# A two-layer graph network on one core: three more tiles of the last block columns kept in SBUF during the first sweep

## The chip, the cores and the metric

The kernel runs on one core of a Trainium2 chip. The metric is device time in microseconds of one execution, as the median of several runs. TensorE (PE) multiplies, VectorE (DVE) and ScalarE (ACT) work on SBUF and PSUM, the queues of SyncE (SP) and GpSimd (POOL) issue the DMA transfers.

## What is computed

```python
x = layernorm(x + layer0(x)); x = layernorm(x + layer1(x))          # x is 8192 x 128
# layer0: d = adj.sum(1); s = 1/(sqrt(d)+1e-8); (adj * s[:,None] * s[None,:]) @ (x@W0 + b0)
# layer1: a = adj + eye;  s = 1/sqrt(a.sum(1)); relu((a * s[:,None] * s[None,:]) @ (x@W1) + b1)
```

`adj` is 8192 x 8192 in float32 (268 MB). Both layers scale it by the degrees of its rows and columns, so a product with column j of the matrix needs the degree of row j first, and layer 1 needs the normalised rows that layer 0 makes.

## The kernel before

**Tiles.** The matrix is cut into 16 x 16 tiles of 512 x 512 (1 MB each), called (i, j). Row i is read in order of i in sweep 1. All tiles of the upper triangle are read again in sweep 2 and all others in sweep 3: 256 + 120 + 136 loads, whatever the constants are.

**Sweep 1** sums the rows for the degrees and multiplies for layer 0 what it can, in f32 (L659). A left tile (j < i) finds its features ready. A tile at or right of the diagonal has to wait until the degree of row j is known. Some are held for that: `held(j)` is min(j, NEAR[j]), so with NEAR = 3 the diagonal tile of column j and the three above it stay in SBUF and are multiplied, by `scaled_takes(j)`, after row j is complete and two tiles of row j + 1 are done. `early(i, j)` says whether a tile is a left tile or a held one. The tiles further right are *far*: ACT only adds them up (L711), from the layout `adj_far`, and their slot is free again. DVE sums all others (L817), folds the row (L824, L827), TensorE turns the sums (L595), and DVE and ACT make the scale and then the features of the row (L835 to L856).

**Sweep 2** goes over the rows from 14 down to 0, each from the last column to the one right of the diagonal. A take of layer 1 (`right1`) needs x1 of row j, the output of layer 0; a far tile is multiplied for layer 0 too (`late0`), in the same take. ACT casts each half of a tile to a high float32r part (L702), DVE makes the low part (L806), and TensorE multiplies three times for each quarter (L683, L684, L685): 12 matmuls for one layer, 24 for both. **Sweep 3** does the left and diagonal tiles for layer 1, and writes the output. I call the takes of sweep 2 t0, t1 and so on: t0 is (14, 15), t1 and t2 are (13, 15) and (13, 14), t6 is (11, 15), t10 and t11 are (10, 15) and (10, 14), t15 is (9, 15).

**From layer 0 to layer 1.** For each row from 15 down: its sums come to SBUF, by ACT's copy out of the bank (L739) if no far tile is outstanding, else the part of sweep 1 was stored in DRAM by L534, is loaded again (L549), and the rest is added by DVE (L872). Rows with a far tile are `late_rows`, here 11 to 0. TensorE turns the sums (`turn0`, L607), DVE makes h and its moments (L884 to L786), ACT the root (L744), DVE x1 (`make_x1`, L774 to L795), TensorE turns x1 (`turn1`, L618), ACT copies it (L747), TensorE multiplies by the weights (`features1`, L626), ACT makes the high part of the features (L751) and DVE the low part (L900). `split_high` and `split_low` (L718, L864) split the f32 features of layer 0, column by column, before the first far tile of that column comes.

**Order.** The class `Plan` writes out the order of each engine's work before the kernel is built: every operation has a key, in units of loads, and each engine runs its list sorted by key; all engines are in-order. `pe_before[u]` is what TensorE does ahead of take u. `turn0[i]` stands 2 takes behind the last product of the row's sums and at least 2 behind the turn before it, `turn1[i]` 3 takes behind `turn0[i]`, the features one further, none later than its first use. PSUM has 6 banks for sums; a group of sums holds its bank from its first take until it is copied out, and `held_before` says which load was in a slot before. Sweep 1 has 19 slots for tiles, 3 of its own (`own`) and 16 that lie where features and rings of later sweeps come (`lent`); sweep 2 only has the 3, and the casts have a ring of 4 halves, so the cast of a take waits until the take two before it is multiplied.

Of the kernel before, what the change touches and what calls it, by code (L numbers as in the profile page):

```python
# [9 lines left out]
NB = N // T  # L10
TILE = Q * T
HALF = TILE // 2
HQ = Q // 2
NEAR = [3] * NB
FAR_PARTS = 4
OWN_SLOTS = 3
LENT1_SLOTS = 16
# [17 lines left out]
def held(j):  # L35

    return min(j, NEAR[j])

# [940 lines left out]
```

How the kernel before makes its waits and increments, by code:

```python
        @block.sync  # L493
        def _(sp):
            sp.dma_start(w_sb[:, :], w0).then_inc(const_landed, 16)
            sp.dma_start(b_sb[:, :], b0.partition_broadcast(P)).then_inc(const_landed, 16)
            for n, (sweep, i, j) in enumerate(loads):
                if sweep < 2 and n % NB == 0:
                    if i >= 2:
                        sp.wait_ge(mixed0_done, i - 1)
                    sp.dma_start(x_t[:, i % 2, :], x_cols[:, i * T:(i + 1) * T]).then_inc(x_t_landed[i % 2], 16)
                m = plan.held_before[n]
                if m is not None:
                    if loads[m][0] == 0:
                        sp.wait_ge(far_summed, plan.far_summed[m])
                    elif loads[m][0] == 1:
                        sp.wait_ge(tile_summed, plan.summed[m])
                        sp.wait_ge(halves_used, 2 * plan.take_of[m] + 2)
                    else:
                        sp.wait_ge(low_ready, 2 * (plan.take_of[m] - plan.natives) + 2)
                elif plan.slot[n] >= OWN_SLOTS + LENT1_SLOTS:
                    sp.wait_ge(halves_used, 2 * plan.lent_again + 2)
                source = adj_far[plan.far_summed[n] - 1] if sweep == 0 else adj_tiles[i, j]
                sp.dma_start(raw(n), source).then_inc(tile_landed[plan.slot[n]], 16)
# [11 lines left out]
            def stored(layer, i):  # L526
                m = stage_at[("empty_right1" if layer else "empty_early0", i)]
                pool.wait_ge(sums_stored[m % 2], 16 * (m // 2 + 1))
```

## Time and profile before

| what | before |
|---|---|
| median of 3 runs | 1884.1 us (1882.98 to 1884.22) |
| the profiled execution | 1884.51 us, span 1882.3 us, mean clock 0.964 |
| TensorE busy | 1655.4 us (88%) |
| TensorE weight loads | 1117.6 us (59%) |
| DVE busy | 1264.2 us (67%) |
| ACT busy | 739.5 us (39%) |
| DMA | 573.38 MB, mean 305 GB/s |

A row of the chain or of the timeline gives the start, the duration and what ran, with how many instructions are merged; in brackets stands how long the engine had been idle and what ended it. PEclk is the granted TensorE clock as a share of full speed. Busy times of matmuls overlap, since they are pipelined.

### The profile page before, as it was taken

The numbers are of one execution on the slowest core, as the hardware profiler recorded it, in microseconds if no ns is written. First come the engines' busy times: TensorE is split into PE (matmuls) and PEld (weight loads), VectorE is DVE, ScalarE is ACT, GpSimd is POOL, SyncE is SP. The second block draws the span as 40 slices with busy tenths as digits, with TensorE's granted clock in tenths as the row PEclk, the third lists the DMA queues.
The fourth block names the chain that finished last, engine by engine and source line by source line (L and its number), as shares of the span: only waits on it lengthen the run. The fifth ranks groups of instructions, "written<-read, shape, count | busy, mean of one in ns | idle before, by whom it ended". The sixth has DMA issues, their size and how long they took to land.

```text
span 1882.3 us, 17109 instructions
## 1 busy us (share of the span) xinstructions
PE 1655.4 (88%) x6136; PEld 1117.6 (59%) x6136; DVE 1264.2 (67%) x1854; ACT 739.5 (39%) x889; POOL 66.2 (4%) x127
## 2 busy tenths in 40 slices
PE   0257889999999999968999999999999999999996
PEld 0123344444444444456777777787787787777775
DVE  1444556776876567277655656545547899999996
ACT  5553342111000000045444444444446666666663
POOL 0000000000000000000000000000000000000000
PEclk9778899999999999989999999999999999999998
DMA  9999999998877976155666665656567999999991
GB/s 387 421 421 421 421 422 393 416 404 343 366 312 290 367 298 232 28 213 212 250 232 227 229 227 209 213 219 228 196 216 313 421 397 363 353 356 361 362 367 78
DMA packets 85906, 573.38 MB, mean 305 GB/s; under 512 B 10400, under 2 KB 10656, under 8 KB 20288
## 3 DMA queue, kind: packets, MB, share of 16 engines
q1 hardware_dynamic: 76320, 541.23, 72.6%
q0 software_dynamic: 9504, 31.07, 4.7%
q8 instruction: 50, 0.82, 0.2%
q14 instruction: 32, 0.26, 0.0%
HBM read 556.79 MB, written 15.47 MB: 304 GB/s over the span
## 4 chain that ended last, share of the span: by engine, by line
PE 67%; DVE 18%; DMA 11%; issue 3%; ACT 1%; SPq 0%; DVEq 0%; POOL 0%; ACTq 0%
PE acc L659 28%; PE acc L683 12%; PE acc L685 12%; PE acc L684 12%; DVE low L806 7%; DMA lent<-adj_tiles 6%; DMA own<-adj_tiles 2%; DVE stats L781 1%; DMA own<-adj_far 1%; DMA lent<-adj_far 1%; DVE run L817 1%; DVE o L795 1%; PE turned L595 1%; DVE z L930 1%; DVE h L884 1%
## 5 line engine op out<-in xcount | busy, mean ns | idle before, releaser
L683 PE MATMUL acc<-high,feat_high 128*128 128x512 f32 x1336 | 536.1, 401 | 70.6 <-DVE low L806 59.5
L659 PE MATMUL acc<-lent,feat 128*128 128x512 f32 x1168 | 522.8, 607 | 20.9 <-DVE feat L856 13.5
L685 PE MATMUL acc<-high,feat_low 128*128 128x512 f32 x1336 | 526.7, 394 | 0.0
L684 PE MATMUL acc<-low,feat_high 128*128 128x512 f32 x1336 | 525.9, 394 | 0.0
L806 DVE TENSOR_TENSOR low<-own,high 128x1024 fp32r<-128x1024 f32 x330 | 390.5, 1220 | 177.7 <-ACT high L702 175.1
L702 ACT CAST high<-own 128x1024 fp32r<-128x1024 f32 x330 | 338.2, 1052 | 197.1 <-PE acc L685 190.4
L659 PEld LDWEIGHTS acc<-lent,feat 128*128 128x128 f32 x1168 | 226.2, 195 | 304.5 <-issue 288.6
L817 DVE TENSOR_TENSOR run<-run,lent 128x2048 f32<-128x2048 f32 x135 | 309.3, 2291 | 135.8 <-DMA lent<-adj_tiles 129.7
L683 PEld LDWEIGHTS acc<-high,feat_high 128*128 128x128 f32 x1336 | 254.1, 190 | 139.2 <-issue 81.5
L685 PEld LDWEIGHTS acc<-high,feat_low 128*128 128x128 f32 x1336 | 254.0, 190 | 55.2
L684 PEld LDWEIGHTS acc<-low,feat_high 128*128 128x128 f32 x1336 | 254.5, 191 | 50.1
L806 DVE TENSOR_TENSOR low<-lent,high 128x1024 fp32r<-128x1024 f32 x182 | 211.8, 1219 | 3.9 <-ACT high L702 2.0
L702 ACT CAST high<-lent 128x1024 fp32r<-128x1024 f32 x182 | 186.3, 1051 | 54.6 <-PE acc L685 52.9
L711 ACT ACTIVATE lent<-lent 128x2048 f32<-128x2048 f32 (+3 forms) x80 | 118.0, 1475 | 74.8 <-DMA lent<-adj_far 73.9
L722 ACT ACTIVATE root<-deg 128x8 f32<-128x8 f32 x16 | 3.3, 209 | 300.4 <-DVE deg L837 300.4
L731 ACT COPY stage<-acc 128x512 f32<-128x512 f32 x27 | 15.8, 586 | 260.7 <-PE acc L659 206.4
L595 PE MATMUL turned<-ones,rowsum 128*128 128x1 f32 x128 | 20.9, 284 | 108.1 <-DVE rowsum L827 108.1
L659 PE MATMUL acc<-own,feat 128*128 128x512 f32 x256 | 115.1, 600 | 0.0
L595 PEld LDWEIGHTS turned<-ones,rowsum 128*128 128x128 f32 x128 | 20.4, 243 | 109.7 <-DVE rowsum L827 67.4
L659 PEld LDWEIGHTS acc<-own,feat 128*128 128x128 f32 x256 | 48.9, 192 | 60.4 <-issue 60.4
L835 DVE TENSOR_REDUCE far<-far_parts 128x4 f32<-128x16 f32 x16 | 2.7, 169 | 108.7 <-PE turned L595 108.7
L817 DVE TENSOR_TENSOR run<-run,own 128x2048 f32<-128x2048 f32 x27 | 61.9, 2291 | 17.5 <-DMA own<-adj_tiles 15.8
(77 smaller groups left out, 649.3 us busy)
## 6 DMA issues: line engine op xcount, KB each, us to landing
lent<-adj_tiles SPq DMA_DIRECT2D x237, 1024.0 KB, 11.1
own<-adj_tiles SPq DMA_DIRECT2D x197, 1024.0 KB, 5.6
lent<-adj_far SPq DMA_DIRECT2D x60, 1024.0 KB, 23.0
own<-adj_far SPq DMA_DIRECT2D x18, 1024.0 KB, 23.0
x_in<-x_rows POOLq DMA_DIRECT2D x32, 256.0 KB, 4.4
sums_rows<-stage POOLq DMA_DIRECT2D x27, 256.0 KB, 6.4
sums_in<-sums_rows POOLq DMA_DIRECT2D x27, 256.0 KB, 6.3
x_t<-x_cols SPq DMA_DIRECT2D x16, 256.0 KB, 15.6
```

Of the source, the lines that this page charges most:

```text
L595: mm = nc.tensor.matmul(turned[:, q:q + 1], rowsum[:, q * P:(q + 1) * P], ones[:, :], start=True, stop=True)
L659: mm = nc.tensor.matmul(bank, feat0[:, j * Q + q, :], raw(n)[:, q * T:(q + 1) * T], start=(u == plan.first[g] and q == 0), stop=(u == plan ...
L683: nc.tensor.matmul(bank, f_high, a_high[:, chunk], start=(u == plan.first[g] and q == 0), stop=False)
L684: nc.tensor.matmul(bank, f_high, a_low[:, chunk], start=False, stop=False)
L685: mm = nc.tensor.matmul(bank, f_low, a_high[:, chunk], start=False, stop=(u == plan.last[g] and q == Q - 1))
L702: nc.scalar.copy(high(m), raw(n)[:, half * HALF:(half + 1) * HALF])\
L711: ins = nc.scalar.activation(piece, piece, ACT.Copy, accum_out=far_parts[:, r, q, k:k + 1])
L781: ins = nc.vector.bn_stats(stats[:, q, :], h[:, q, :])
L795: ins = nc.vector.tensor_scalar(dst[:, q, :], h[:, q, :], moments[:, q, 0:1], rstd[:, q:q + 1], ALU.subtract, ALU.mult)
L806: nc.vector.tensor_tensor(low(m), raw(n)[:, half * HALF:(half + 1) * HALF], high(m).bitcast(F32), ALU.subtract).then_inc(low_ready, 1)
L817: ins = nc.vector.tensor_tensor(run[:, :], run[:, :], raw(i), ALU.add)
L884: ins = nc.vector.scalar_tensor_tensor(out=h[:, q, :], in0=turned_q[:, q, :], scalar=scale[:, i, 0, q:q + 1], in1=x_in[:, r, q, :], op0=AL ...
```

## The change

One constant: the last two block columns hold four and five tiles above their diagonal.

```diff
-NEAR = [3] * NB
+NEAR = [3] * (NB - 2) + [4, 5]
```

So (10, 14), (10, 15) and (11, 15) are held and multiplied in sweep 1 by L659, summed by DVE and loaded in the layout of the other tiles, and in sweep 2 they are takes of layer 1 alone. Everything that `Plan` derives from `held`, `early` and `far_width` follows: rows 10 and 11 have no far tile and are no `late_rows`, their turns have other places, and `split_high` and `split_low` of columns 15 and 14 come before t13, beside those of column 13. The number of loads in all stays.

## Rows read from the trace of the kernel before

**Rows 1.** The page: the chain by engine, and three of its costliest groups.

```profile
PE 67%; DVE 18%; DMA 11%; issue 3%; ACT 1%; SPq 0%; DVEq 0%; POOL 0%; ACTq 0%
...
L683 PE MATMUL acc<-high,feat_high 128*128 128x512 f32 x1336 | 536.1, 401 | 70.6 <-DVE low L806 59.5
L659 PE MATMUL acc<-lent,feat 128*128 128x512 f32 x1168 | 522.8, 607 | 20.9 <-DVE feat L856 13.5
...
L817 DVE TENSOR_TENSOR run<-run,lent 128x2048 f32<-128x2048 f32 x135 | 309.3, 2291 | 135.8 <-DMA lent<-adj_tiles 129.7
```

**Rows 2.** The chain in order of time: start, us, what; row 15 of sweep 1.

```profile
713.50 65.34 PE acc L659 x152
```

**Rows 3.** Stretches: length, busy PE, PEld, DVE, ACT, POOL, then PEclk, DMA share, GB/s.

```profile
808.04:893.96 85.92, 67.00 (x281) 52.69 (x281) 60.99 (x153) 40.24 (x64) 7.50 (x14) 0.89 0.58 210
893.96:914.51 20.55, 20.55 (x97) 17.08 (x98) 11.39 (x14) 10.35 (x15) 1.18 (x3) 1.00 0.67 254
340.18:778.84 438.66, 438.66 (x1107) 200.94 (x1107) 299.27 (x270) 27.32 (x52) 4.32 (x8) 1.00 0.78 314
```

**Rows 4.** DVE at the degrees of rows 10 and 11; SP's waits, 440 to 480 us.

```profile
479.79 0.17 DVE L835 TENSOR_REDUCE far<-far_parts 128x4 f32<-128x16 f32 x1 [3.60 <-PE turned L595]
...
533.08 0.17 DVE L835 TENSOR_REDUCE far<-far_parts 128x4 f32<-128x16 f32 x1 [9.94 <-PE turned L595]
...
SPq L508 <- PE acc L659: 36.9, 8, 16.8
```

**Rows 5.** TensorE where sweep 1 ends and t0 begins.

```profile
800.63 0.60 PE L607 MATMUL turned<-ident,sums_in 128*128 128x128 f32 x4
801.07 0.60 PE L618 MATMUL mixed<-ident,x 128*128 128x128 f32 x4
...
808.04 0.77 PE L683 MATMUL acc<-high,feat_high 128*128 128x512 f32 x1 [3.38 <-issue]
```

**Rows 6.** ACT's first cast and DVE's steps in the first takes of sweep 2.

```profile
800.91 1.99 ACT L702 CAST high<-own 128x1024 fp32r<-128x1024 f32 x2 [4.06 <-PE acc L659]
...
801.99 2.36 DVE L806 TENSOR_TENSOR low<-own,high 128x1024 fp32r<-128x1024 f32 x2 [2.76 <-ACT high L702]
804.27 1.12 DVE L884 SCALAR_TENSOR_TENSOR h<-turned,scale,x_in 128x128 f32<-128x128 f32 x4
...
806.82 1.12 DVE L900 SCALAR_TENSOR_TENSOR feat_low<-mixed,scale,feat_high 128x128 fp32r<-128x128 f32 x4
...
814.30 0.17 DVE L774 TENSOR_SCALAR sdev<-sdev 128x4 f32<-128x4 f32 x1 [4.10 <-ACT sdev L744]
...
816.56 2.35 DVE L806 TENSOR_TENSOR low<-own,high 128x1024 fp32r<-128x1024 f32 x2
...
848.95 2.36 DVE L806 TENSOR_TENSOR low<-own,high 128x1024 fp32r<-128x1024 f32 x2 [5.11 <-ACT high L702]
```

**Rows 7.** TensorE: row 14's x1, t2, t5, t6, t11, features, t15, row 9.

```profile
816.79 0.63 PE L618 MATMUL mixed<-ident,x 128*128 128x128 f32 x4 [0.39 <-DVE x L795]
...
822.56 0.50 PE L683 MATMUL acc<-high,feat_high 128*128 128x512 f32 x1 [3.30 <-DVE feat_low L900]
...
841.62 0.79 PE L683 MATMUL acc<-high,feat_high 128*128 128x512 f32 x1 [4.28 <-DVE feat_low L900]
...
846.91 0.40 PE L683 MATMUL acc<-high,feat_high 128*128 128x512 f32 x1
...
873.35 0.48 PE L683 MATMUL acc<-high,feat_high 128*128 128x512 f32 x1
...
878.92 1.05 PE L626 MATMUL mixed<-w_sb,x_t 128*128 128x128 f32 x8
...
893.96 0.47 PE L683 MATMUL acc<-high,feat_high 128*128 128x512 f32 x1 [1.52 <-DVE low L806]
...
914.51 0.60 PE L607 MATMUL turned<-ident,sums_in 128*128 128x128 f32 x4
```

**Rows 8.** Loads of sweep 2 between 800 and 960 us: median time from issue to landing.

```profile
own<-adj_tiles SPq DMA_DIRECT2D x28, 1024.0 KB, 4.9
```

## The prediction

> **What bounds the kernel now.** I read the page's chain and its costliest groups first [rows 1], then the chain in order of time [rows 2], then busy time by stretch [rows 3], and last the instructions of the stretch in which the stages meet [rows 5 to 7]. The chain is two thirds TensorE, with f32 matmuls (L659) ahead of the float32r ones (L683 to L685), so both kinds of matmul that the change trades lie on the path [rows 1]. From 340 to 779 us TensorE is busy all of 438.66 us, DVE 299.27, and the DMA moves at 0.78 of its share: the second part of sweep 1 is bound by TensorE, and what is added there lengthens the kernel in full [rows 3]. Sweep 2 begins at 808 us, and its first 86 us are another matter. TensorE is busy 67.0 us of 85.9 at a mean clock of 0.89; DVE is busy 61.0 us [rows 3]. That stretch holds takes t0 to t14 of sweep 2 (t0 is the tile (14, 15)), 18 tile products with the three that count for both layers. The stalls there come from the chain that makes x1 and its features row by row, and from the in-order queues of ACT and DVE [rows 6, 7]. From t15 on, TensorE is nearly full again: all of 20.55 us [rows 3].
>
> **Prices.** Mean durations of matmuls overlap and can't be multiplied. A row of sweep 1 gives the pitch: 152 instructions, which are 19 tiles, take 65.34 us, so a tile product in f32 is 3.44 us [rows 2]. A tile that serves both layers in sweep 2 takes 878.92 - 873.35 = 5.57 us for 24 matmuls, so one layer's product is 2.79 us at the full clock [rows 7]. Behind a pause of 4.28 us the 12 matmuls of t5 took 846.91 - 841.62 = 5.29 us, 0.44 each instead of 0.23: that is the lower of the clock's two levels, 1.2 against 2.4 GHz [rows 7]. The page's means (607 and about 400 ns) would price the trade at 24 x 0.607 = 14.6 against 36 x 0.40 = 14.4 us [rows 1]. The Trainium skill, Perfetto Trace Analysis, section Identifying the Most-Contended Engine, says that matmul busy time is a bad measure because matmuls are pipelined; the trace agrees, since 152 x 0.607 = 92 us of duration fit in 65 us. The skill's page TensorE: Matmul & The Clock Gate, section "Wait — 56ns, not 53.3ns?", gives 215.7 ns from start to start for 512 columns at 2.4 GHz; by it 36 matmuls would be 7.8 us where the rows give 8.4, and the sum would be 0.6 us worse; the trace has 232 ns here.
>
> **What sweep 1 pays.** Tiles (10,14), (10,15) and (11,15) now are multiplied there: 3 x 3.44 = 10.3 us of TensorE, all of it on the path [rows 2, 3]. (10,14) joins the products of row 14's columns inside row 15; the two others come last of all. In the order of the plan, the turn of row 14's sums and that of row 15's x1 now come ahead of the last products, where before they followed them: two groups of four, from 800.63 to 801.07 each 0.44 us, together 0.9 us [rows 5]. The last f32 product (I call these native) thus ends 11.2 us later (800.63 + 11.2 = 811.8). DVE sums three more tiles (2.29 us each), ACT three fewer; DVE waits for TensorE 3.60 us at the degree of row 10 and 9.94 us at that of row 11, so I cost this at nothing; without that cover it is 6.9 us [rows 1, 4].
>
> **Slots.** The three tiles occupy 3 of the 19 slots that hold left tiles and prefetches otherwise. A slot less can make the last load of a row wait for one more product, 3.44 us. The loads wait for TensorE anyway (SP: 36.9 of 40 us), so what counts is how long a row is folded before its degree is needed: about 4 us at row 10 and 10 us at row 11, where DVE waits for TensorE [rows 4], and more at each row after. Two slots fewer in row 10 are 6.9 against 4 us, so 3 us of stall at most; three in row 11 are 10.3 against 10. But two far tiles fewer pass through the ring in row 10, and the burst of its last loads still starts when the held column before it is released. I take 0, with 0 and 3 us as bounds, and nothing below 0, since no earlier landing helps a busy TensorE.
>
> **What sweep 2 gets: the order.** Three takes of t0 to t14 lose one of two products: 8.4 us if TensorE set the pace. But rows 10 and 11 also are no longer late. Their sums stay in banks instead of going out and back: two stores and two loads leave POOL's queue, two adds DVE's, and two copies move on ACT from sweep 1 to behind the casts of t3 and t5, where they wait for nothing. Their turns move from before t8 and t13 to before t4 and t6, and all of x1 down to row 10 comes earlier in every queue: x1 of row 14 is made under the last products of sweep 1, and features of row 10 come before t10 instead of t17. The splits of columns 15 and 14 move from before t4 and t8 to before t13, beside that of column 13. The banks suffice (rows 10 to 15 take all six; sweep 2 opens on banks that are emptied by copies under the last products).
>
> **The walk.** I placed each operation in the new order of its queue, with the spacings of the trace: ACT's pair of high casts 1.9 us, its start 1.08 us ahead of DVE's lows; the lows 2.3; h with its moments 2.55; x1 from sdev 2.25; the low part of the features 1.05 [rows 6]; from a turn to the first use of its features 5.8 us with DVE busy between (816.79 to 822.56), which I take as 4.9 where it isn't [rows 7]. With 0 at the end of the last native product: t0 starts at 7.4 as before (808.04 - 800.63), for DVE still has one low pair, one h and one feature group before it. t2 stays at 21.9: its features stand behind the same work. From there the chain is one row ahead. t2 ends at 26.6 (slow clock, as before); x1 of row 13 is turned there, t3 ends at 29.8, its features' product at 31.2, their high part on ACT at 32.5; DVE has x1 of row 12 to 30.1, t4's lows to 32.4, h of row 11 to 34.9, row 13's low part to 36.0 and then t5's lows, so t5 starts at 37.4 (before: 41.0). In the same way t6 starts at 42.3 (46.3), t7 at 47.8, t8 at 52.4, t9 at 55.7, t10 at 59.4, t12 at 66.0, and t15, behind the three splits, at 75.3 (893.96 - 800.63 = 93.3) [rows 5, 7]. Of these 18.0 us, 8.4 are the products and 9.6 are stalls and slow clock. In it DVE would be busy 63 of 73 us, which is what is late next: t6 to t14 wait for DVE's lows, not for x1. From t15 to the turn of row 9 another 1.4 us go (0.44 for row 10's turn, 0.9 for its features) [rows 7]; after it the order is that of before. Casting needs the tiles: SP may load a tile once the low of three takes earlier is done, and it lands 4.9 us later; my walk leaves 4.2 to 7.4 us, so t14's cast may be 1.5 us late, under DVE work [rows 8].
>
> Sum: 10.3 + 0.9 - 18.0 - 1.4 = -8.2 us. The profiled execution had a span of 1882.3 and a time of 1884.51 us; the median is 1884.1, 0.4 lower. Forecast 1884.1 - 8.2 = 1875.9 us. For the walk I allow 5 us to either side: it rests on 60 small spacings, and its floor is DVE's 10 us of idle time, which could fall away too (-18 in all, 1866).
>
> **Rivals.** *The trade alone.* Only the products count: 10.3 - 8.4 = +1.9, 1886.0 us. For it: t2 doesn't move in my walk. Against it: TensorE loses about 30 us in t0 to t14 (85.9 less 18 x 2.79 = 50.2 for products, less some 6 for turns and features) [rows 3], in seven pauses and the slow matmuls behind them; two of the pauses stand in [rows 7].
> *Half of the chain's gain.* DVE's order costs what the earlier x1 brings: the clump of three splits before t13 (1.8 us on DVE) and the earlier h of row r - 2 ahead of row r's features hold takes up. Then some 5 us of 9.6 are left, 1880.5 us.
> *The chain decides, slower.* If x1 and its features on ACT and DVE set t0 to t14, products taken away there save nothing and sweep 1 still pays: 11.2 - 1.4 = +9.8, 1893.9 us. It decides for slower by over 0.2% as soon as t0 to t14 shorten by less than 6 us. For it: t0, t2 and t5 start right behind features that DVE finished [rows 7]. Against it: DVE is idle 25 of 86 us there [rows 3], and lows of it wait for ACT, whose casts stand behind takes not yet done (5.11 us before t7's) [rows 6].
> *Slots.* Stalls in rows 10 to 13: +3 us on my forecast, 1879; they alone don't turn the sign.
> *It isn't done.* If loads or late rows stayed as they are, nothing would move; the rule for early tiles reads the constant directly, so 1 in 100.
>
> **How the numbers follow.** This kernel's runs lie within 1.2 us, and about 0.2% (3.8 us) can be told from no change. My forecast with its slots case 0.61 (1871 to 1880.3), a gain still larger 0.06, half the gain 0.13, the trade alone 0.09, slower by the chain or by both chain and slots 0.10, not done 0.01. Half the gain falls on both sides of 1880.3: half of it counts as faster, so faster 0.61 x 0.95 + 0.06 + 0.06 = 0.70, same 0.18, slower 0.12 (a part of the trade alone among it). The range runs from 1870 to 1887: it takes in half the gain, the slots and the trade alone, and leaves out 0.1 above and 0.06 below.
>
> **What would show it.** The f32 stretch of row 15 has 160 instructions instead of 152, six tiles instead of four stand behind it, the last native product ends near 812, and t0 starts 7.4 us behind it; an earlier start would mean more gain. The turn of row 9 should start about 8 us sooner than 914.5. Two L872 and two L549 fewer; L659 x1448 in all, 36 float32r matmuls fewer. The 4.28 us stall for row 13's features becomes about 3, and idle DVE in the stretch to t15 falls from 25 to about 10 us. Wrong would be: a gap of TensorE at a degree (L595) in rows 10 to 13, or t15 later than 80 us behind the last native product. If the stages after row 9 differ by more than 1 us, I have missed something altogether.

## The result, and the profile after

| what | before | after |
|---|---|---|
| median of 5 runs each, on the same chip | 1884.22 us (1882.98 to 1884.94) | 1877.32 us (1874.38 to 1879.53) |
| ratio, 95% interval | | 0.9963 (0.9949 to 0.9978) |
| profiled execution, span | 1882.3 us | 1872.3 us (its time is 1874.38 us) |
| mean TensorE clock | 0.964 | 0.966 |

The change makes the kernel 6.9 us faster by the medians and 10.0 us by the two profiled executions. The forecast was 8.2. The profiled execution of after is the fastest of its five, so the first thing to find out is which part of the 10.0 belongs to the change.

The page of after answers to [rows 1]: the chain by engine, and three groups. L659 now has 1168 + 280 = 1448 instructions, 36 fewer float32r matmuls run (L683, L684 and L685 have 12 fewer each), and L549 and L872 have 10 instead of 12.

```profile
PE 67%; DVE 18%; DMA 10%; issue 3%; SPq 1%; ACT 0%; DVEq 0%; POOL 0%; ACTq 0%
...
L683 PE MATMUL acc<-high,feat_high 128*128 128x512 f32 x1324 | 529.0, 400 | 65.7 <-DVE low L806 54.9
L659 PE MATMUL acc<-lent,feat 128*128 128x512 f32 x1168 | 532.1, 614 | 18.5 <-DVE feat L856 13.5
...
L659 PE MATMUL acc<-own,feat 128*128 128x512 f32 x280 | 125.2, 593 | 0.0
```

The chain of after in order of time, through sweep 1. Row 10 starts behind row 9's degree, row 11 behind row 10's, and so on. The last of the long stretches is that of row 15, which answers to [rows 2]: 160 instructions for 152. Behind the degree of row 15 stand 16, 16, 8 and 8 instructions of the last columns, which are six tiles where before has four.

```profile
428.00 48.17 PE acc L659 x112
...
477.86 51.61 PE acc L659 x120
...
531.14 55.04 PE acc L659 x128
...
711.60 68.77 PE acc L659 x160
...
785.44 9.91 PE acc L659 x16
...
795.79 6.87 PE acc L659 x16
...
803.09 3.44 PE acc L659 x8
...
806.97 3.45 PE acc L659 x8
```

DVE at the degrees of rows 10 and 11, which answers to [rows 4]. DVE still waits for TensorE there (before: 3.60 and 9.94 us), so no degree is late.

```profile
477.89 0.17 DVE L835 TENSOR_REDUCE far<-far_parts 128x4 f32<-128x16 f32 x1 [3.78 <-PE turned L595]
...
531.18 0.17 DVE L835 TENSOR_REDUCE far<-far_parts 128x4 f32<-128x16 f32 x1 [7.42 <-PE turned L595]
```

TensorE of after from the last native product, which ends at 810.24, on. These rows answer to [rows 5] and [rows 7]: t0, t2, the turn of row 12's x1, t5, t6, t7, t8, t14, and the turn of row 9's sums.

```profile
810.24 0.60 PE L607 MATMUL turned<-ident,sums_in 128*128 128x128 f32 x4
...
817.65 0.77 PE L683 MATMUL acc<-high,feat_high 128*128 128x512 f32 x1 [5.92 <-DVE feat_low L900]
...
831.90 0.70 PE L683 MATMUL acc<-high,feat_high 128*128 128x512 f32 x1 [4.82 <-DVE feat_low L900]
...
845.85 0.66 PE L618 MATMUL mixed<-ident,x 128*128 128x128 f32 x4 [1.63 <-DVE feat_low L900]
...
847.07 0.47 PE L683 MATMUL acc<-high,feat_high 128*128 128x512 f32 x1 [0.57 <-DVE low L806]
...
851.60 0.47 PE L683 MATMUL acc<-high,feat_high 128*128 128x512 f32 x1 [0.22 <-DVE low L806]
...
857.45 0.47 PE L683 MATMUL acc<-high,feat_high 128*128 128x512 f32 x1 [0.56 <-DVE low L806]
...
861.98 0.47 PE L683 MATMUL acc<-high,feat_high 128*128 128x512 f32 x1 [0.65 <-DVE low L806]
...
882.61 0.47 PE L683 MATMUL acc<-high,feat_high 128*128 128x512 f32 x1 [1.40 <-DVE low L806]
...
904.49 0.60 PE L607 MATMUL turned<-ident,sums_in 128*128 128x128 f32 x4
```

Stretches of after, with the columns of [rows 3]: t0 to t14, t15 to the turn of row 9, and from there to the end of the span. The first took 85.92 us before, at a clock of 0.89.

```profile
817.65:885.30 67.65, 55.09 (x252) 43.98 (x253) 56.20 (x132) 40.84 (x66) 5.98 (x11) 0.94 0.70 253
885.30:904.40 19.10, 19.10 (x86) 15.83 (x85) 10.36 (x10) 10.47 (x11) 0.55 (x1) 1.00 0.74 283
904.49:1872.30 967.81, 899.62 (x4061) 734.09 (x4059) 712.72 (x1161) 511.06 (x565) 46.27 (x85) 0.99 0.73 277
```

**Where the 10.0 us went.** Cut each span at three points: H, the start of TensorE's turns (L595) at the degree of row 9; E, the end of the last native product; and G, the start of the turn of row 9's sums. From G to the end both kernels take 967.8 us (1882.3 - 914.51 and 1872.3 - 904.49): nothing behind row 9 differs. From H to G before takes 914.51 - 428.95 = 485.56 us and after 904.49 - 427.05 = 477.44 us, so 8.12 us less. (H is read from the timeline of TensorE; in the chain the eight turns start 0.16 us later in both kernels.) The other 1.9 us lie ahead of H, where the engines of both kernels run the same instructions (the loads differ only in their order from row 10 on, fetched in advance). The experiments below show that H moves by itself, so I compare H to G everywhere.

### The profile page after: what moved, and what is told of

Same layout as the page of the kernel before. It is cut to its first block, busy times and chain, and to the rows that moved or that the text cites. A ratio compares the mean times of both kernels' runs of the same rounds, so it can differ in the third digit from the quotient of the medians.

```text
span 1872.3 us, 17067 instructions
## 1 busy us (share of the span) xinstructions
PE 1657.6 (89%) x6124; PEld 1114.2 (60%) x6124; DVE 1270.5 (68%) x1855; ACT 733.4 (39%) x873; POOL 64.3 (3%) x123
## 4 chain that ended last, share of the span: by engine, by line
PE 67%; DVE 18%; DMA 10%; issue 3%; SPq 1%; ACT 0%; DVEq 0%; POOL 0%; ACTq 0%
PE acc L659 29%; PE acc L683 12%; PE acc L684 12%; PE acc L685 12%; DVE low L806 7%; DMA lent<-adj_tiles 5%; DMA lent<-adj_far 3%; DMA own<-adj_tiles 2%; DVE stats L781 1%; SPq L514 1%; DVE o L795 1%; DVE z L930 1%; PE turned L595 1%; DVE h L884 1%; DVE run L817 1%
## 5 line engine op out<-in xcount | busy, mean ns | idle before, releaser
L683 PE MATMUL acc<-high,feat_high 128*128 128x512 f32 x1324 | 529.0, 400 | 65.7 <-DVE low L806 54.9
L659 PE MATMUL acc<-lent,feat 128*128 128x512 f32 x1168 | 532.1, 614 | 18.5 <-DVE feat L856 13.5
L685 PE MATMUL acc<-high,feat_low 128*128 128x512 f32 x1324 | 520.3, 393 | 0.0
L684 PE MATMUL acc<-low,feat_high 128*128 128x512 f32 x1324 | 519.8, 393 | 0.0
L659 PEld LDWEIGHTS acc<-lent,feat 128*128 128x128 f32 x1168 | 228.5, 197 | 304.8 <-issue 288.2
L683 PEld LDWEIGHTS acc<-high,feat_high 128*128 128x128 f32 x1324 | 250.9, 190 | 133.0 <-issue 78.8
L685 PEld LDWEIGHTS acc<-high,feat_low 128*128 128x128 f32 x1324 | 250.9, 189 | 54.1
L684 PEld LDWEIGHTS acc<-low,feat_high 128*128 128x128 f32 x1324 | 251.1, 190 | 49.0
L711 ACT ACTIVATE lent<-lent 128x2048 f32<-128x2048 f32 (+3 forms) x72 | 111.4, 1548 | 74.0 <-DMA lent<-adj_far 73.3
L659 PE MATMUL acc<-own,feat 128*128 128x512 f32 x280 | 125.2, 593 | 0.0
L595 PE MATMUL turned<-ones,rowsum 128*128 128x1 f32 x128 | 20.6, 282 | 103.7 <-DVE rowsum L827 103.7
L659 PEld LDWEIGHTS acc<-own,feat 128*128 128x128 f32 x280 | 53.0, 190 | 66.0 <-issue 66.0
L595 PEld LDWEIGHTS turned<-ones,rowsum 128*128 128x128 f32 x128 | 20.1, 239 | 105.3 <-DVE rowsum L827 63.0
L817 DVE TENSOR_TENSOR run<-run,own 128x2048 f32<-128x2048 f32 x31 | 71.0, 2291 | 14.6 <-DMA own<-adj_tiles 13.2
```

The source lines that it names most:

```text
L595: mm = nc.tensor.matmul(turned[:, q:q + 1], rowsum[:, q * P:(q + 1) * P], ones[:, :], start=True, stop=True)
L659: mm = nc.tensor.matmul(bank, feat0[:, j * Q + q, :], raw(n)[:, q * T:(q + 1) * T], start=(u == plan.first[g] and q == 0), stop=(u == plan ...
L683: nc.tensor.matmul(bank, f_high, a_high[:, chunk], start=(u == plan.first[g] and q == 0), stop=False)
L684: nc.tensor.matmul(bank, f_high, a_low[:, chunk], start=False, stop=False)
L685: mm = nc.tensor.matmul(bank, f_low, a_high[:, chunk], start=False, stop=(u == plan.last[g] and q == Q - 1))
L711: ins = nc.scalar.activation(piece, piece, ACT.Copy, accum_out=far_parts[:, r, q, k:k + 1])
```

## The experiments

Times in us. The last columns are the median, what it is above (+) or below (-) the median of before on the same chip, and the ratio of the two.

| kernel | H to E | E to t0 | E to G | H to G | median | to before | ratio (95%) |
|---|---|---|---|---|---|---|---|
| before | 371.69 | 7.40 | 113.87 | 485.56 | 1884.22 |  | |
| after | 383.19 | 7.41 | 94.25 | 477.44 | 1877.32 | -6.90 | 0.9963 (0.9949 to 0.9978) |
| after_again | 383.44 | 7.41 | 96.62 | 480.06 | 1877.12 | -7.64 | 0.9958 (0.9946 to 0.9971) |
| late_all | 381.86 | 7.42 | 105.88 | 487.74 | 1887.04 | +2.28 | 1.0012 (1.0003 to 1.0021) |
| late_turns | 382.56 | 7.41 | 107.89 | 490.45 | 1889.39 | +5.12 | 1.0025 (1.0015 to 1.0035) |
| only_10_14 | 375.01 | 7.40 | 111.19 | 486.20 | 1885.64 | +1.37 | 1.0006 (0.9997 to 1.0015) |
| only_11_15 | 375.48 | 7.26 | 103.80 | 479.28 | 1879.40 | -5.83 | 0.9969 (0.9957 to 0.9980) |
| half_products | 376.96 | 7.65 | 94.67 | 471.63 | 1870.62 | -13.65 | 0.9928 (0.9914 to 0.9942) |
| low_first | 381.90 | 4.86 | 94.31 | 476.21 | 1872.84 | -12.39 | 0.9940 (0.9928 to 0.9953) |
| low_first3 | 383.41 | 4.85 | 88.61 | 472.02 | 1870.19 | -14.57 | 0.9919 (0.9906 to 0.9933) |
| before_low_first | 370.65 | 6.46 | 110.08 | 480.73 | 1881.79 | -3.44 | 0.9985 (0.9976 to 0.9994) |
| splits_early | 382.93 | 7.41 | 94.51 | 477.44 | 1875.32 | -9.91 | 0.9954 (0.9941 to 0.9966) |
| four_slots | 383.47 | 4.86 | 86.95 | 470.42 | 1867.34 | -17.42 | 0.9904 (0.9891 to 0.9918) |

fewer_slots is no variant of the change and is told of below.

One profile can't be read to a tenth here. after and after_again are the same kernel and differ by 2.6 us from H to G, nearly all of it behind E. Ahead of E the 16 instructions behind row 15's degree, some of them at the lower clock, take between 8.62 us (low_first) and 10.20 us (four_slots) in six profiles whose instructions are the same up to there. So where H to G differs by less than 3 us, the medians have to bear it out.

**The trade without the order: late_turns and late_all.** My theory: the products alone cost about 2 us, and the gain comes from the order, since rows 10 and 11 are no late rows and turns move ahead. The rival is that the freed products carry the gain. late_turns keeps the three tiles and puts the six turns back to where before has them.

```diff
+LATER = {15: -2, 14: 0, 13: 2, 12: 4, 11: 8, 10: 13}
...
+            if i in LATER:
+                before = self.turn0[i] = self.last[("early0", 10)] + 1 + LATER[i]
```

> The changed kernel, with the turns, x1 and features of rows 15 to 10 put back to the places (counted from the first take of sweep 2) that they have in the kernel before; the three tiles stay in sweep 1. My theory (about 10 us of the gain is the order): 3 x 3.44 us more in sweep 1, 8.4 us fewer products in sweep 2, so about +2 us against the kernel before, 1886, and t15 starts some 85 us behind the last native product. Rival 'the chain decides' (products save nothing there): up to 1894, t15 at 93. Rival 'the order brings nothing': as the changed kernel, 1877, t15 at 75.

It is slower than before: +4.9 us from H to G and +5.1 by the medians. That is more than the trade, and the trace says why. The splits of columns 15, 14 and 13 still come together. They push the last low parts ahead of t14 back, and behind the pause the matmuls run at 0.43 us each: the splits on DVE of late_turns, then its TensorE at t14, and the turn of row 9.

```profile
891.23 1.89 DVE L867 TENSOR_TENSOR feat_low<-feat,feat_high 128x512 fp32r<-128x512 f32 x3
...
894.40 0.77 PE L686 MATMUL acc<-high,feat_high 128*128 128x512 f32 x1 [3.63 <-DVE low L809]
894.96 0.63 PE L687 MATMUL acc<-low,feat_high 128*128 128x512 f32 x1
895.39 0.63 PE L688 MATMUL acc<-high,feat_low 128*128 128x512 f32 x1
...
920.43 0.60 PE L610 MATMUL turned<-ident,sums_in 128*128 128x128 f32 x4
```

late_all puts the splits of columns 15 and 14 back too (their `at` is set to their old loads), so that its turns and splits stand where before has them, with after's tiles. Rows 10 and 11 still keep their sums in their banks, as in after.

```diff
 (late_turns, and)
+            at = {15: 260, 14: 264}.get(j, at)
```

> As late_turns, and the splits of columns 15 and 14 at their places of the kernel before as well, so that only the products are traded. In late_turns a pause of 3.63 us and slow matmuls stood ahead of t14, behind the clump of splits. If the clump made it: 2 to 3 us less than late_turns, so +2 to +3 against the kernel before, 1886.5. If the waits come from the chain alone: as late_turns, 1889.4.

The same place in late_all: one split instead of three, a pause of 2.46 us, and no slow matmuls behind it.

```profile
887.60 0.68 DVE L868 TENSOR_TENSOR feat_low<-feat,feat_high 128x512 fp32r<-128x512 f32 x1
...
889.56 0.47 PE L687 MATMUL acc<-high,feat_high 128*128 128x512 f32 x1 [2.46 <-DVE low L810]
...
914.63 0.60 PE L611 MATMUL turned<-ident,sums_in 128*128 128x128 f32 x4
```

So the trade of the products alone is +2.2 us from H to G (+10.17 to E, -7.99 from E to G), +2.3 by the medians. late_turns takes 2.7 us more than that from H to G, of which 0.7 lie ahead of E, where the two run the same instructions; the other 2.0 (2.8 by the medians) are the price of the clump of splits where it meets a late x1. The intervals of the two ratios still meet (1.0015 to 1.0035 and 1.0003 to 1.0021). The order brings 487.74 - 477.44 = 10.3 us, or 9.9 by the medians of late_all and after_again on one chip (7.7 by after_again's profile).

**One part at a time: only_10_14 and only_11_15.** One tile is (10, 14), whose row 10 stays late for (10, 15); the other kernel takes (11, 15) alone, and with it row 11 is no longer late.

```diff
-NEAR = [3] * (NB - 2) + [4, 5]
+NEAR = [3] * (NB - 2) + [4, 3]     # only_10_14
+NEAR = [3] * (NB - 2) + [3, 4]     # only_11_15
```

> Only column 14 holds one tile more, so (10,14) is the only product that moves; rows 10 and 11 stay late and no turn changes its place. A clean trade: +3.44 us in sweep 1, -2.8 us in sweep 2 where TensorE sets the pace at t11. My theory: +0.6 us, 1884.8. Rival 'the chain decides': +3.4, 1887.6. Rival 'each tile brings a third of the gain': -2.3, 1881.9.

+0.64 us from H to G, and the stalls are those of before one for one (3.38, 3.31 and 4.29 us ahead of t0, t2 and t5). H to E grows by 3.32 us, and E to G shrinks by 2.68: the price of one product of each kind, within 0.12 us of 3.44 and 2.79. By the medians it is +1.4, with an interval that takes in no change. A tile whose row stays late is a trade that brings nothing. It isn't quite alone, against what I had expected: row 10's last far product is now t10, so that its turn comes one take sooner, and the split of column 14 stands beside that of column 13.

> Only column 15 holds one tile more, (11,15). Row 11 leaves the late rows and the turns of rows 15 to 11 come one take earlier (11: three takes), row 10 stays late. In sweep 1 +3.44 +0.44 us. If products alone count: +1.1, 1885.4. If the earlier turns bring it, more than a third of the whole gain shows with a third of the products: 1880 to 1882.

-6.3 us of the 8.1 (-5.8 by the medians), from one tile. It is the row that matters, not the number of tiles: row 11's sums stay in their bank, and the turns of rows 15 to 12 move ahead by one take and that of row 11 by three.

**Whether f32 products are hidden: half_products.** In the three moved products only two of the four quarters are multiplied, which leaves out half of each.

```diff
-                    for q in range(Q):
+                    for q in ((HQ - 1, Q - 1) if (i, j) in ((10, 14), (10, 15), (11, 15)) else range(Q)):
```

> The changed kernel, but of the three moved tiles only two of the four column blocks are multiplied in sweep 1 (the other half of these products is left out). If f32 products at the end of sweep 1 lie on the path in full: 3 x 1.72 = 5.2 us less than the changed kernel, 1872. If the last two are hidden beside the x1 of row 15: 1.7 us less, 1875.6.

-5.8 us against after from H to G. Half of three products is 5.16 us. H to E shortens by 6.23 us, 1.08 of it because the start of the last columns ran less of its time at the slow clock (in the chain, 8.83 us for 16 instructions instead of 9.91, which lies within the scatter named above), and E to G is 0.4 longer. By the medians it is 6.0 to 6.7 us below after. The products lie on the path in full, as the 10.17 us of late_all say.

**Slots: fewer_slots.** The kernel before with three lent slots fewer.

```diff
-LENT1_SLOTS = 16
+LENT1_SLOTS = 13
```

> The kernel before with 13 lent slots instead of 16, so 16 in all: it takes away what the three held tiles take, in every row. My theory: the rows from 10 on are still folded ahead of their degree, within 1 us of 1884.2; the DMA-bound rows ahead of 340 us may lose some us, which the changed kernel doesn't. Rival 'slots': a stall of TensorE at the degree of row 10, 3 us, perhaps at 11 too, 1887 or more with no loss ahead of 340 us.

1915.88 us, ratio 1.0167 (1.0153 to 1.0181): far more than the 3 us that I gave as a bound, but in another place. Stretches from the start to the degree of row 9, of before and then of fewer_slots (columns of [rows 3]):

```profile
0.00:429.11 429.11, 297.60 (x755) 142.57 (x755) 231.45 (x263) 158.92 (x205) 4.36 (x13) 0.90 1.00 412
```

```profile
0.00:460.30 460.30, 303.62 (x755) 145.79 (x755) 231.63 (x263) 159.46 (x205) 4.37 (x13) 0.88 0.94 383
```

The DMA, which is the bound of this stretch, is no longer full: 383 instead of 412 GB/s, and the same bytes take 31 us more. From the start of row 10's products to the last columns both take 354.0 us (815.07 - 461.07 and 783.89 - 429.90). So slots are worth much where transfers are the bound and nothing from row 10 on, which is the only part where the three tiles occupy them. The rival of the slots was wrong for this change.

**The next stall: low_first, low_first3 and before_low_first.** t0, t2 and t5 of after start right behind the low part of the features (L900), which stands behind lows and h in DVE's list. low_first moves it ahead of them for all rows; low_first3 for rows 15 to 13 alone; before_low_first is low_first on before.

```diff
-            dve.append((lo_key(k2, 8), "features1_low", i))
+            dve.append((lo_key(k2, 2), "features1_low", i))                        # low_first, before_low_first
+            dve.append((lo_key(k2, 2 if i >= NB - 3 else 8), "features1_low", i))  # low_first3
```

> The changed kernel, but DVE makes the low part of a row's features (L900) ahead of the next row's h and moments (L884 to L786), not behind them. If t0 and t2 start when DVE gets to those features (my reading: 1.2 us behind them), t0 comes 2.5 us sooner, t2 about 5 us sooner, and from t4 on DVE is full, so no more is won: 5 to 6.5 us less than the changed kernel, about 1871.5. Rival 'DVE is full anyway': the same time, 1877.3, since the order of a full engine gives nothing.

t0 starts 2.55 us earlier, and at t6 6.1 us are won behind E (847.05 - 811.82 = 35.23 where after has 41.36), but at G nothing is left of it in this profile: 94.31 us from E to G, where after takes 94.25. The 1.2 us that H to G is shorter lie ahead of E, where the edit changes nothing (8.62 us for the 16 instructions instead of 9.91). DVE of low_first, and TensorE behind it:

```profile
848.51 1.12 DVE L900 SCALAR_TENSOR_TENSOR feat_low<-mixed,scale,feat_high 128x128 fp32r<-128x128 f32 x4 [1.60 <-ACT feat_high L751]
```

```profile
853.47 0.77 PE L683 MATMUL acc<-high,feat_high 128*128 128x512 f32 x1 [2.96 <-DVE low L806]
854.03 0.63 PE L684 MATMUL acc<-low,feat_high 128*128 128x512 f32 x1
```

In the later rows the high part of the features isn't made yet when DVE gets there. DVE, in order, stands still, its next low is late, and the clock falls. Where DVE has the slack the early place helps; where it is late next, it hurts. But the profiled execution is the slowest of five (1876.52 us; the others took 1872.00 to 1874.62), and by the medians low_first is 12.4 us below before where after is 6.9 and 7.6 below. So this trace shows how the gain can be lost again; by the medians some 5 us of it stay.

> The changed kernel, with the low part of the features first for rows 15, 14 and 13 alone, where it stood in DVE's way; for rows 12 to 10 as before, because in low_first DVE then stood and waited 1.6 to 2.4 us for ACT's high part and lost all it had won (5.8 us at t6). Expected: t6 5.8 us sooner and the turn of row 9 5 us sooner than in the changed kernel, 1872. If the loads set t10 to t14 (its casts waited 2.55 us for one): the lead melts to 0 to 2 us, 1876.

-5.4 us against after from H to G, ratio 0.9919: the gain is kept when the rows that made DVE wait are left where they were. Against low_first that is 4.2 us in the profiles and 2.2 by the medians, on two chips and with intervals that meet at 0.993, so the harm of the later rows is shown in one trace and only likely in the medians.

> The same edit on the kernel before. If the gain of the three tiles is a way round this one place in the order, the kernel before gains as much or more by it, 8 to 12 us, to 1874 to 1876, and little is left to the tiles. If the tiles' gain is that x1 of rows 14 to 10 is made earlier altogether, it gains some 5 us, 1879, and low_first stays about 8 us ahead of it.

-4.8 us against before from H to G, 3.8 of it behind E, and -3.4 by the medians. So a good part of what the tiles bring in this stretch was to be had from the order alone; the two gains are no substitutes, since low_first3 adds its own to the tiles'.

**What stands behind t14: splits_early and four_slots.** splits_early moves the splits of the last three columns up to the first takes, where DVE is idle.

```diff
+            if j >= NB - 3:
+                k = self.natives + (1 if j > NB - 3 else 3)
+                act.append((hi_key(k, 0.6 - j / 100), "split_high", j))
+                dve.append((lo_key(k, 0.6 - j / 100), "split_low", j))
+                continue
```

> The changed kernel, with the splits of columns 15, 14 and 13 taken out of their clump before t13 and put into DVE's and ACT's idle time behind t1's and t3's lows. Rival 'the clump costs': 1.9 us less, 1875.4. My reading of the trace after: the cast of t14 waits 2.55 us for its load, which its slot lets start only behind t11's low, so t14 starts when it does now: 0 to -0.5 us, 1877.

477.44 us, that of after (to the hundredth by chance: the two parts differ by 0.26 us in opposite directions). ACT of after and then of splits_early ahead of t14's cast:

```profile
880.15 2.00 ACT L702 CAST high<-own 128x1024 fp32r<-128x1024 f32 x2 [2.55 <-DMA own<-adj_tiles]
```

```profile
880.96 1.99 ACT L707 CAST high<-own 128x1024 fp32r<-128x1024 f32 x2 [3.04 <-DMA own<-adj_tiles]
```

The cast waits that much longer for its load, which lands 69.9 and 70.2 us behind E: with the splits away, the three slots of sweep 2 set t14. The medians leave more open. splits_early's, 1875.32 us, is what the rival of the clump had (1875.4), 9.9 us below before where after is 6.9 and 7.6 below, with intervals that overlap widely (0.9941 to 0.9966, 0.9946 to 0.9971). That the splits cost nothing in after is shown for the profiled executions alone.

four_slots is after with low_first3, splits_early and a fourth slot.

```diff
-OWN_SLOTS = 3
+OWN_SLOTS = 4
...
-            top[0] += -(-nbytes // 64) * 64
+            top[0] += -(-nbytes // 32) * 32
...
-        far_parts = put("far_parts", [P, NB, Q, FAR_PARTS])
+        far_parts = put("far_parts", [P, NB - 5, Q, FAR_PARTS])
...
-                    then(nc.vector.tensor_reduce(far[:, :], far_parts[:, i, :, :], AX.X, ALU.add))
+                    then(nc.vector.tensor_reduce(far[:, :], far_parts[:, min(i, NB - 6), :, :], AX.X, ALU.add))
```

> The changed kernel with a fourth own slot for tiles, which fits when small tensors are packed more tightly and far_parts drops rows that have no far tile, with low_first3 and the early splits. Three slots fewer cost 31 us ahead of row 9's degree, so one more should bring 3 to 10 us there; in t10 to t14 the casts should no longer wait for loads, and the turn of row 9 should come 6 to 9 us sooner behind the last native product. In all about 1866. If the head is bound by DMA bandwidth alone (421 GB/s through it): nothing there, 1870.

The fastest of all: 1867.34 us (1866.29 to 1867.64), ratio 0.9904, 17.4 us below before and 9.8 below after (1884.76 and 1877.12 on the same chip). From H to G it is 7.0 below after, 1.6 of that beyond low_first3 (2.9 by the medians). No run has the slot without the early splits, so that part belongs to both together; the wait of t14's cast for its load was 3.19 us in low_first3. ACT's one remaining wait for a load there, and the stretch up to the degree of row 9:

```profile
875.07 2.01 ACT L707 CAST high<-own 128x1024 fp32r<-128x1024 f32 x2 [1.07 <-DMA own<-adj_tiles]
```

```profile
0.00:426.90 426.90, 303.05 (x754) 144.04 (x754) 231.52 (x263) 159.05 (x205) 4.38 (x13) 0.90 1.01 417
```

A gain ahead of H, which I expected, isn't to be seen beyond the scatter: the DMA was full before (412 GB/s at a share of 1.00) and is full now. The Trainium skill, DMA: Bandwidth & Descriptors, section Specifications, gives 435 GB/s as the ceiling of the fabric for a core; the trace agrees, with 417 GB/s here over the whole stretch.

**The scatter: after_again.** The kernel after, unchanged, once more.

> The changed kernel, unchanged, beside the others of this batch. In the traces so far the rows ahead of row 9's degree took 427.0 to 430.9 us with the same instructions, the rest agreed to some tenths. If that part only scatters: again 1874 to 1880, median near 1877.3, and a head that differs from the 427.05 us of the first trace. If the change shortened the head: a head of 427 again.

H is 428.93 instead of 427.05, and G comes 2.4 us later after E. ACT and TensorE of after_again at t14:

```profile
883.07 1.99 ACT L702 CAST high<-own 128x1024 fp32r<-128x1024 f32 x2 [3.24 <-DMA own<-adj_tiles]
```

```profile
885.52 0.70 PE L683 MATMUL acc<-high,feat_high 128*128 128x512 f32 x1 [2.08 <-DVE low L806]
886.02 0.63 PE L684 MATMUL acc<-low,feat_high 128*128 128x512 f32 x1
```

The load of t14 lands later (3.24 us of waiting for 2.55), t14 starts 0.78 us later behind E, and its first eight matmuls take 3.5 us (885.52 to 889.01) where after's take 1.8. That is 0.8 + 1.7 us, the 2.4 within what the rows resolve.

## Why the prediction was right, point by point

**Sweep 1 pays 11.2.** Measured 11.5 (383.19 - 371.69). The trade is 10.17 of it (late_all), and 1.33 is the two moved turns (0.88) and more slow clock at the last columns: 16 instructions took 9.91 us where before took 9.59. The term was right; the 0.3 that it is short is less than this place scatters by itself. half_products shows that it is paid in full.

**Slots 0.** Right in the sign and the size for rows 10 to 13: the chain shows each row's products run through at 3.43 to 3.44 us a tile, and DVE waits for TensorE at every degree. The bound of 3 us was for the right rows. Three slots in the rows ahead of them cost ten times as much, which I would have missed had the change touched those.

**The walk, -18.0 and -1.4.** Positions behind the last native product:

| | t0 | t2 | t5 | t6 | t7 | t8 | t15 | turn of row 9 |
|---|---|---|---|---|---|---|---|---|
| forecast | 7.4 | 21.9 | 37.4 | 42.3 | 47.8 | 52.4 | 75.3 | 94.5 |
| after | 7.41 | 21.66 | 36.83 | 41.36 | 47.21 | 51.74 | 75.1 | 94.25 |

The forecast of the turn is 113.87 - 18.0 - 1.4. t15 of after is t14's start and its 12 matmuls, 882.61 + 2.73 - 810.24. No position is off by more than 1 us, and t0 didn't move, as said. Row 13's features cost 1.63 + 0.57 us of waiting where the walk had 3; that was the one stall that came out smaller. DVE is idle 67.65 - 56.20 = 11.4 us to t15, where I gave 10. From t8 on the releaser of each pause is DVE's low, as forecast, but ahead of t14's low stood a load: the 1.5 us that I let pass "under DVE work" are the 2.55 us on ACT. They didn't cost the forecast anything in the profiled run; in after_again, with 3.24 us of waiting, t14 came later than in after.

**The split of the gain.** The forecast had +1.9 for the products and -10.1 for the order (+0.9 for turns, -9.6 for stalls and slow clock, -1.4 for row 10 behind t15). The runs give +2.2 and -10.3 (+2.3 and -9.9 by the medians). The rival of the trade alone was thus right about the trade's price (1886.0; late_all has 1887.0) and wrong that the order does nothing. *Half of the chain's gain* named the clump of three splits as the taker. late_turns shows that the clump can cost 2.0 us, but splits_early shows 0 in the profile of after, where x1 is early; its median leaves up to 2 us open. *The chain decides* fell: t0 to t14 shortened by 18.3 us (85.92 to 67.65), far beyond the 6 that decide.

**The sum.** -8.2 forecast, -8.12 from H to G in the profiled executions. That they agree to 0.1 us is luck: after_again gives -5.5, and the medians -6.9 and -7.6. The measured times scatter for reasons that I hadn't in the sum. H lies anywhere from 426.8 to 430.9 us in the thirteen profiles of all kernels but fewer_slots, though the instructions up to it are the same, t14 comes with or without 2.4 us, and the first 16 instructions behind row 15's degree take 8.6 to 10.2 us. The profiled run of after had an early H and no slow matmuls at t14; the median of five is 1877.3, 1.4 above the forecast. That these places make all of the 5 us between after's fastest and slowest run is argued from the profiles, not shown. The five runs of before here lie within 2 us, but that isn't its width: 15 others on one chip lie between 1883.08 and 1888.90.

## What to carry to other kernels

A swap of work of nearly equal price can still pay when it takes a whole row (or block) out of a slow path: ask of each moved tile whether it is the last that keeps its row there, for one such tile brought 6.3 us and one that wasn't brought nothing (+0.6, within the noise). Compare kernels between two fixed points of the trace (here H and G) before reading their spans, since a transfer-bound start can move by 4 us without any edit; and take a second profile of the same kernel before reading a difference of 2 us, and look where the profiled execution lies among its runs. An operation moved ahead in an in-order engine's list helps only as far as its inputs are there; where they aren't, it holds up everything behind it.

## What the runs showed of the hardware

- The length of the last pause alone doesn't tell whether the TensorE clock falls. Slow matmuls, 0.43 us each, stood behind pauses of 2.08 us (after_again, t14), 2.54 and 2.96 us (low_first, t5 and t7), and none behind 2.46 us (late_all, t14), 2.39 and 3.37 us (low_first, t2 and t0). The same kernel went both ways at one place: at t20, the pause is 1.81 us in after and in after_again, and eight of after's matmuls are slow and none of after_again's. The fourth and fifth matmul of t20, in after and then in after_again:

```profile
910.42 0.52 PE L683 MATMUL acc<-high,feat_high 128*128 128x512 f32 x1
910.75 0.63 PE L684 MATMUL acc<-low,feat_high 128*128 128x512 f32 x1
```

```profile
914.93 0.40 PE L683 MATMUL acc<-high,feat_high 128*128 128x512 f32 x1
915.16 0.39 PE L684 MATMUL acc<-low,feat_high 128*128 128x512 f32 x1
```

- The clock's rise varies too: behind a pause of 5.92 us ahead of t0, the first nine matmuls are slow in after and the first ten in after_again. The Trainium skill, TensorE: Matmul & The Clock Gate, section What you observe, says that the point of the change to the fast clock varies from run to run; the trace agrees, with these nine and ten.
- With three of 19 slots of 1 MB fewer, a stretch bound by transfers ran at 383 instead of 412 GB/s (31 us of 429). With one more than 19 it ran at 417, and its end, H at 426.8 us, is no sooner than the 426.9 of late_all with 19.
- Transfers at the full DMA share took between 426.8 and 430.9 us up to H in profiles whose instructions up to there are the same.
